# Linear attention whose keys' exponentials are taken from the turned context, with outputs one step behind their sums, and feed-forward scales moved into its middle steps

## The reference

```python
# stage 1: q from x (normalized), k and v from the context
qh = softmax(qh, axis=3)                     # over the 32 channels of a head
kh = softmax(kh, axis=1)                     # over the 1024 positions
kvs = einsum('bnhd,bnhe->bhde', kh, vh)
out = einsum('bnhd,bhde->bnhe', qh, kvs)     # x = x + tanh(g_xattn[0]) * out
# stage 2: feed-forward with 4-bit weights and low-rank parts
y1 = x1 @ Wg + x1 @ g_lora_a @ g_lora_b ; y2 = x1 @ Wu + x1 @ u_lora_a @ u_lora_b
x3 = relu(y1) * y2 ; y3 = x3 @ Wd + x3 @ d_lora_a @ d_lora_b
# stages 3 and 4: auto-correlation attention and a linear layer
```

## Time and profile before

| | us |
|---|---|
| median of 3 runs | 2186.99 (2183.91 to 2187.79) |
| profiled execution | 2186.56 |
| its span | 2184.8 |
| PE busy | 2050.8 (94%) |
| ACT busy | 1176.9 (54%) |
| DVE busy | 1094.9 (50%) |
| POOL busy | 663.8 (30%) |

### The profile page before, as it was taken

One profiled execution on the slowest core, in us unless ns is written; L12 is line 12 of the kernel. 1 busy time (PEld: TensorE's weight loads), 2 busy tenths in 40 slices (PEclk: granted clock), 3 DMA queues, 4 the chain that ended last, 5 costly groups with the idle time before them and its releaser, 6 DMA issues. The chain is left out here.

```text
span 2184.8 us, 25848 instructions
## 1 busy us (share of the span) xinstructions
PE 2050.8 (94%) x9634; PEld 1022.4 (47%) x9634; DVE 1094.9 (50%) x1935; ACT 1176.9 (54%) x1843; POOL 663.8 (30%) x640
## 2 busy tenths in 40 slices
PE   7986999999999999999999999999865799999997
PEld 5773444444444444444444444444322455555543
DVE  6774252433425243342524234252546788888862
ACT  6994756556565655656566565657122344443421
POOL 3432212112121211212121111212125666677641
PEclk9997999999999999999999999999876899999999
DMA  6632211121111112111111111110300011111000
GB/s 224 201 121 68 64 49 54 49 64 49 49 54 50 54 50 63 49 49 54 56 50 54 55 49 49 54 58 20 121 29 10 29 39 49 49 46 37 25 27 31
DMA packets 58493, 128.37 MB, mean 59 GB/s; under 512 B 8704, under 2 KB 9344, under 8 KB 58368
## 3 DMA queue, kind: packets, MB, share of 16 engines
q1 hardware_dynamic: 58368, 126.72, 18.1%
HBM read 118.30 MB, written 8.39 MB: 58 GB/s over the span
## 5 line engine op out<-in xcount | busy, mean ns | idle before, releaser
L664 ACT ACTIVATE first<-first 128x512 f32<-128x512 int32 x1008 | 632.7, 628 | 28.0
L896 PE MATMUL ps_ring<-xT_hi,gu_hi 128*128 128x512 f16 x1376 | 522.1, 379 | 1.7 <-POOL gu_lo L736 1.7
L896 PE MATMUL ps_ring<-xT_hi,gu_lo 128*128 128x512 f16 x1376 | 521.9, 379 | 0.0
L896 PE MATMUL ps_ring<-xT_lo,gu_hi 128*128 128x512 f16 x1376 | 521.8, 379 | 0.0
L805 DVE SCALAR_TENSOR_TENSOR X<-ps_ring,ffn_gain,X 128x512 f32<-128x512 f32 x352 | 259.9, 749 | 168.9 <-PE ps_ring L919 168.8
L786 DVE SCALAR_TENSOR_TENSOR wt<-first,w_scale,absm 128x512 f32<-128x512 f32 x132 | 98.8, 749 | 479.1 <-ACT first L664 478.1
L736 POOL TENSOR_TENSOR gu_lo<-wt,gu_hi 128x512 f16<-128x512 f32 x88 | 102.6, 1166 | 746.7 <-ACT gu_hi L670 746.7
L919 PE MATMUL ps_ring<-dn_hi,hid_hi 128*128 128x512 f16 x704 | 270.0, 384 | 0.0
L919 PE MATMUL ps_ring<-dn_hi,hid_lo 128*128 128x512 f16 x704 | 269.7, 383 | 0.0
L919 PE MATMUL ps_ring<-dn_lo,hid_hi 128*128 128x512 f16 x672 | 256.4, 382 | 0.0
L896 PEld LDWEIGHTS ps_ring<-xT_hi,gu_lo 128*128 128x128 f16 x1376 | 134.5, 98 | 163.1 <-issue 0.8
(11 more groups left out here) (203 smaller groups left out, 2673.4 us busy)
## 6 DMA issues: line engine op xcount, KB each, us to landing
first<-in_codes SPq DMA_DIRECT2D x132, 256.0 KB, 2.8
absm<-in_absmax SPq DMA_DIRECT2D x264, 128.0 KB, 3.1
X<-in_x SPq DMA_DIRECT2D x16, 512.0 KB, 4.1
c_in<-in_ctx SPq DMA_DIRECT2D x16, 512.0 KB, 5.0
cT<-in_ctxT SPq DMA_DIRECT2D x16, 512.0 KB, 3.5
xT_hi<-in_ctx SPq DMA_DIRECT2D x8, 1024.0 KB, 7.2
out<-X SPq DMA_DIRECT2D x16, 512.0 KB, 3.3
gu_hi<-in_w SPq DMA_DIRECT2D x8, 512.0 KB, 3.6
```

Source lines behind the costliest of these rows:

```text
L664: act.activation(level[u % 2][:], codes[u % RING] if k == 0 else level[u % 2][:], ACT.Prelu, bias=bias, scale=scale, alpha=alpha).then_inc ...
L896: mm = pe.matmul(o[:], w[c][:, m, k, :], xx[:, k, ts], start=(q == 0), stop=(q == 3 * KD - 1))
```

## The change

- Keys: the maximum cm goes to PE, which spreads it over all partitions (`maxima`), ACT copies it out (cmx), POOL subtracts it from the turned context (`less_max`, new, 128x1024), and ACT takes the exponentials straight into ekT (`keys`). The eight turns of ek and the copy to ekT are gone. The key sums come from a column of ones behind each block of cT, as column 128 of the product.
- The head sums of eq take four columns of blk for each block, and lie in psE. The turned inverse sums have a buffer rT of their own, and eq has three copies.
- POOL multiplies eq in the step after its sums (`eqn` of tile i-1 in step i). DVE forms the second offset of tile i-2 in step i, after xT_lo and ahead of rS; `prepare` is split, and the first offset stands at the end of the step. ACT's xn is one step later too.
- The scales' parts move: squares in step 7, reductions in step 8, PE and DVE gathering in steps 9 and 10, POOL's roots in step 11, DVE's chain in step 12; their loads are issued ahead of tile 4.

```diff
 pool_part:  -        if i == TILES:
             +        if i == AT + 3:                       # AT = 8
 act_part:   -        if i == TILES - 2:
             +        if i == AT - 1:
 dve_part:   -        if i == TILES - 1:   +        if i == AT:
             -        if i == TILES:       +        if i == AT + 1: (top, diag)  and  if i == AT + 2: (every)
             -        if i == TILES + 1:   +        if i == AT + 4:
@@ SP
-                sp.dma_start(cT[h][:], io["ctxT"][b, h]).then_inc(cT_in[h], 16)
+                sp.dma_start(cT[h][:, :, 0:P], io["ctxT"][b, h].rearrange("p (k j) -> p k j", k=KD)).then_inc(cT_in[h], 16)
...
-                        sp.wait_ge(ek_done, b * 2 + h - 1)
+                        sp.wait_ge(cmax_done, b * 2 + h - 1)
@@ POOL
+            def less_max(i, h):
+                pool.wait_ge(cT_in[h], (i // 2) * 16 + 16)
+                pool.wait_ge(cmx_done, i + 1)
+                after(pool, kv_mm, i - 1)
+                pool.tensor_tensor(ekT[h][:].rearrange("p (k j) -> p k j", k=KD), cT[h][:, :, 0:P],
+                                   cmx[h][:].unsqueeze(1).to_broadcast([P, KD, P]), ALU.subtract).then_inc(sub_done, 1)
             def step(i, h):
                 if exists(i - 1):
-                    rsqrt(i - 1, 1 - h, mv2, ve2, rstd2, mv2_done, ve2_done, rstd2_done)
-                if exists(i):
-                    pool.wait_ge(turned_done, i + 1)
-                    pool.tensor_tensor(eq[h][:], rSx[:], eq[h][:], ALU.mult).then_inc(eqn_done, 1)
+                    pool.wait_ge(turned_done, i)
+                    pool.tensor_tensor(eq[(i - 1) % 3][:], rT[:], eq[(i - 1) % 3][:], ALU.mult).then_inc(eqn_done, 1)
+                if exists(i + 1):
+                    less_max(i + 1, 1 - h)
                 if exists(i + 2):
                     rsqrt(i + 2, h, mv, ve, rstd, mv_done, ve_done, rstd_done)
+                if exists(i - 1):
+                    rsqrt(i - 1, 1 - h, mv2, ve2, rstd2, mv2_done, ve2_done, rstd2_done)
...
             for h in range(2):
                 rsqrt(h, h, mv, ve, rstd, mv_done, ve_done, rstd_done)
+            less_max(0, 0)
@@ ACT, new order of step(i): queries(i+1), xn(i-2), maxima(i+1), rSx(i), first_kinks(i), keys(i+1), turned(i) into rT, xT_hi(i-2)
+            def maxima(i, h):
+                act.wait_ge(cmb_mm, i + 1)
+                after(act, sub_done, i - 1)
+                act.activation(cmx[h][:], ps_max, ACT.Copy).then_inc(cmx_done, 1)
+            def keys(i, h):
+                act.wait_ge(sub_done, i + 1)
+                act.activation(ekT[h][:], ekT[h][:], ACT.Exp).then_inc(ek_done, 1)
@@ PE, new order of step(i): sums(i), product(i), maxima(i+1), out(i-1), turned sums(i), xT(i-2)
+            def maxima(i, h):
+                pe.wait_ge(cmax_done, i + 1)
+                after(pe, rS_done, i)
+                pe.matmul(ps_max, cm[h][:].to_broadcast([P, P]), ident[:], start=True, stop=True).then_inc(cmb_mm, 1)
...
+                        mm = pe.matmul(ps_sums[:, k * HR:(k + 1) * HR], eq[i % 3][:, k * P:(k + 1) * P], blk[:, 0:P:ROWS0], start=True, stop=True)
...
+                        mm = pe.matmul(ps_kv, ekT[h][:, k * P:(k + 1) * P], cT[h][:, k, :], start=(k == 0), stop=(k == KD - 1))
@@ DVE
             def prepare(i, h):
+                dve.wait_ge(ctx_in[h], (i // 2) * 16 + 16)
+                after(dve, cmb_mm, i - 1)
+                dve.reduce_max(cm[h][:], c_in[h][:], AX.X).then_inc(cmax_done, 1)
+                dve.wait_ge(x_in[h], (i // 2) * 16 + 16)
                 stats(i, h, st, mv, stats_done, mv_done)
...
             def step(i, h):
                 (xT_lo of tile i-3, as before)
+                if exists(i - 2):
+                    offset(i - 2, h, mv2, rstd2, nmr2, rstd2_done, nmr2_done)
                 if exists(i):
                     dve.wait_ge(sums_mm, i + 1)
+                    dve.reciprocal(rS[h][:], ps_sums).then_inc(rS_done, 1)
+                if exists(i + 2):
+                    prepare(i + 2, h)
+                if exists(i):
+                    dve.wait_ge(kv_mm, i + 1)
+                    dve.reciprocal(rks[h][:], ps_kv[:, P:P + 1]).then_inc(rks_done, 1)
+                    dve.wait_ge(rks_done, i + 1)
+                    dve.scalar_tensor_tensor(kvm[h][:], ps_kv[:, 0:P], rks[h][:], blk[:], ALU.mult, ALU.mult).then_inc(kvm_done, 1)
                 (X and its statistics of tile i-1, as before)
+                if exists(i + 2):
+                    offset(i + 2, h, mv, rstd, nmr, rstd_done, nmr_done)
 
             for h in range(2):
                 prepare(h, h)
+            for h in range(2):
+                offset(h, h, mv, rstd, nmr, rstd_done, nmr_done)
```

More of the change, by code:

```diff
@@ L221, in dve_part, with read, left @@
             dve.wait_ge(step, 30)
-    return sp_part, pool_part, act_part, pe_part, dve_part
+    def read(engine):
+        engine.wait_ge(step, 3)
+    def left(pe, i):
+        if i == AT + 2:
+            pe.wait_ge(step, 7)
+        if i == AT + 3:
+            pe.wait_ge(step, EVERY)
+    return sp_part, pool_part, act_part, pe_part, dve_part, read, left
 def exists(i):
@@ L309, in _ @@
                 for b in range(1, B):
+                    if b == 2:
+                        scales_sp(sp)
                     if b == 3:
@@ L375, in step @@
                 def step(i, h):
-                    if exists(i):
-                        after(act, kv_mm, i - 1)
-                        act.wait_ge(ekT_mm, i + 1)
-                        act.activation(ekT[h][:], psE[:], ACT.Copy).then_inc(ekT_done, 1)
-                    first_kinks(i)
-                    if exists(i):
-                        after(act, eqn_done, i)
+                    if exists(i + 1):
+                        queries(i + 1, 1 - h)
+                    if exists(i - 2):
+                        after(act, xT_mm, i - 3)
+                        act.wait_ge(nmr2_done, i - 1)
+                        settle(act)
+                        act.activation(xn[h][:], X[:, i - 2, :], ACT.Identity, scale=rstd2[h][:], bias=nmr2[h][:]).then_inc(xn_done, 1)
+                    if exists(i + 1):
+                        maxima(i + 1, 1 - h)
+                    if exists(i):
+                        after(act, rS_mm, i)
                         act.wait_ge(rS_done, i + 1)
@@ L401, in step @@
                                        ACT.Copy, scale=LN_SCALE).then_inc(hi_done, 1)
-                exponentials(0, 0)
+                queries(0, 0)
+                maxima(0, 0)
+                keys(0, 0)
                 act.wait_ge(gates_in, 32)
@@ L427, in step @@
                         for n in range(2):
-                            mm = pe.matmul(psO[:, n * BANK:(n + 1) * BANK], kvm[1 - h][:], eq[1 - h][:, n * BANK:(n + 1) * BANK], start=True, stop=True)
+                            mm = pe.matmul(psO[:, n * BANK:(n + 1) * BANK], kvm[1 - h][:], eq[(i - 1) % 3][:, n * BANK:(n + 1) * BANK], start=True, stop=True)
                         mm.then_inc(out_mm, 1)
                     if exists(i):
-                        pe.wait_ge(ekT_done, i + 1)
-                        pe.wait_ge(cT_in[h], (i // 2) * 16 + 16 if isinstance(i, int) else (i - h) * 8 + 16)
-                        for k in range(KD):
-                            mm = pe.matmul(psE[:, 0:P], ekT[h][:, k * P:(k + 1) * P], cT[h][:, k * P:(k + 1) * P], start=(k == 0), stop=(k == KD - 1))
-                        mm.then_inc(kv_mm, 1)
                         pe.wait_ge(rSx_done, i + 1)
+                        after(pe, turned_done, i)
                         for k in range(KD):
@@ L448, in _ @@
                 pe.wait_ge(const_in, 32)
+                pe.wait_ge(ones_set, 2)
+                maxima(0, 0)
                 run(pe, step, scales_pe)
```

119 lines of the change are left out of this document (53 added, 66 removed).

## The result

The changed kernel takes 2214.53 us, the median of four runs (2207.84 to 2219.71). The kernel before took 2187.39 beside it, also of four (2183.91 to 2191.63). The ratio of after to before is 1.0109, with an interval of 1.0085 to 1.0133. The forecast was slower, at 2196, with a range up to 2202: the time is above that range. The kernel did get slower and the held offset is there, but the size is not: the medians are 27 us apart, and the ratio puts the loss at 24 us (19 to 29), where the forecast had 9. The profiled execution is the fastest of the four, at 2207.84.

A forecast was written before the change was run, and what follows sets the result against it. ACT bound the 9.32 us step, PE 0.2 us behind. After: 31.9 to first X addition, 146.7 for steps with scales, 9.9 at the end: 188.5 against 178.6, 9.9 more, rounded to 9.5: 2196 us, range 2182 to 2202.

The forecast's parts named there:

- the held offset: DVE's second offset always falls into POOL's product and is held until its end, 2.30 us instead of 0.16; chance 0.60.
- first X addition: Stage's start: later offset, table load and POOL's subtraction delay the first X addition by about 6.5 us (5.5 to 7.5).
- The ring: Regular step: chain from one POOL product's end through DVE to the next product's end sets the step, 9.7 against 9.32 us.
- the first rival: Regular step: offset not held, ACT sets steps of 8.4 us, stage 173.8 us, time 2182 us; chance 0.18.
- the second rival: In the prediction's list: offset held in some steps only, mean step 9.05 us, time 2188.5 us; chance 0.12.
- PE ... is not the bound and I price this at zero: Regular step: PE's busy time falls below 8 us, so its changed work costs no time.
- the third rival: Subtraction 3.0 us, loads stalling the start, PE longer at half clock there: 2 us each, time 2202 us; chance 0.10.
- The scales: Scales' parts in middle steps: reductions +1.2 us in step 8, roots +1.0 and DVE's chain +2.1 in step 12.
- The loads: Regular step: cT is needed a step earlier but a full step covers its load, priced at zero; uncovered, 1 to 2 us.
- The subtraction: POOL's added 128x1024 subtraction in each regular step takes 2.37 us, with 2.0 and 3.0 as ends.
- fourth rival: PE's head sums with 4 columns do not get shorter; this changes no time in any case, as PE has room.
- The end: From the last X addition to the stage's end: about 9.9 us instead of 12.4, 2.5 less.

The follow-up runs named there:

- the last experiment: The kernel before the change with its offsets in the one-input form (scalar operand) and nothing else changed: 2181.94 us, ratio 0.9973 to the kernel before.

## Why the prediction was right in kind and wrong in size

The forecast put the stage's end at 188.5; the profiled execution has 202.8. Its terms against what was measured:

| term | forecast | measured |
|---|---|---|
| first X addition | +6.5 | +9.5 |
| regular step, held | 9.7 | 9.69 to 9.79 in five of fifteen |
| steps 1, 2 and 5 | 3 x 9.7 | 32.7, so +3.6 |
| steps 8 to 12, over 5 x 9.7 | +4.3 | +9.6 |
| last three steps | 26.0 | 28.0 |
| from last X addition to the end | 9.9 | 10.1 |

The 14.3 us between the two ends can be read from DVE's waits in after, since DVE sets the steps; these sums are estimates from one execution. Waits for PE's output at half clock make about 8: 1.55 ahead of the first addition, 0.98 and 0.45 in steps 2 and 5, 1.8 in step 11, 1.33 in step 12 and 1.8 in step 15. Waits for the context make about 5: the queries' start 1.5 later than forecast, 1.87 in step 1 and 1.70 in step 9. About 1 us is left over.

- **The held offset: right.** The ring came out at 9.70 us against 9.7. With the hold gone the step is 8.57 where the first rival had 8.4 (its time of 2182 did not follow, though: 2207.77, for the reasons below; and the prediction's sentence that calls the unheld case the second rival means this first one), and the comparison in which only the offset's form differs puts the hold's price at 18.4 us of the steps. The Trainium skill's rule ("SBUF — State Buffer", section "Who interferes with whom") fits both: the form with one input in SBUF passes in 0.20 us under a running product, the form with two takes until its end. The scalar operand lies in SBUF too; the traces show only that it does not bring the hold.
- **"PE ... is not the bound and I price this at zero": the step that failed.** It took PE's busy time at full clock. That was so before: PE was busy for 8.54 of 9.32 us, and the granted clock stood at 1.00 from 20 to 160 us. In after it is busy for 7.94 of 9.70. PE's gap ahead of its turn for the maximum grew to 1.8 us in the regular step shown and to 3 us and more around the scales, and the granted clock fell to 0.82 to 0.91 from 100 us on. A group behind a gap then takes up to 1.8 us longer just where it ends the wait of DVE's X. That is in the start (sixteen matmuls in 3.6 to 3.8 us), in the output of steps 11 and 12 (+1.8 and +1.6), and in the last step, 10.33 instead of 8.5. Filling the gaps took the terms of steps 2, 5 and 11 away, but added as much elsewhere, so no run isolates the 8 us. The forecast did say half clock of the last turns, but for the end alone, and the third rival had a longer half clock at the start, at 2 us.
- **The scales: their own work was priced about right.** Steps 8 to 12 came 5.3 us dearer than forecast, by the two causes around this one. The reductions made step 8 longer by 1.0 us, with 1.2 forecast. Step 9 is the wait for the context. Step 11 is 2.9 over 9.7; 1.8 of that is the output's half clock, and 1.1 is left for the roots, with +1.0 forecast, and the offset got through as said (0.15 us at 143.25). Step 12 is 3.8 over; DVE's 1.33 us for PE's output leave 2.5 for the chain, with +2.1 forecast. Its held instruction is a later one (L210) and not its first, as the forecast had it. In the kernels without the hold the same work has less shade: 2.2 us for the reductions (10.8 less 8.58), and 8.6 for roots and chain, some of it clock, against 2.5 and 3.7 in the first rival.
- **The loads: a zero that holds only for a long step.** In after DVE waits 2.35 and 1.05 us for the context ahead of the first addition (before, 1.94 us for tile 1's x), and 1.87 and 1.70 in steps 1 and 9. SP issued these last two loads right behind the scales' inputs (33.01 to 34.18) and behind the low-rank loads (113.48 to 115.11); with the low-rank loads moved away, step 9 has no such wait. Landing times of the profile's DMA part went up from 4.1 to 5.0 us for x, 5.0 to 5.9 for the context and 3.5 to 4.4 for cT:
```profile
DMA packets 72828, 128.35 MB, mean 58 GB/s; under 512 B 8704, under 2 KB 25728, under 8 KB 72704
X<-in_x SPq DMA_DIRECT2D x16, 512.0 KB, 5.0
c_in<-in_ctx SPq DMA_DIRECT2D x16, 512.0 KB, 5.9
cT<-in_ctxT SPq DMA_DIRECT2D x16, 512.0 KB, 4.4
```
  Packets under 2 KB were 9344 before. Once the hold was gone, these waits grew to 12.2 us, and issuing two tiles ahead ended those in the steps. The third rival had the loads, the start and the clock together, at 2 us each; the clock and the loads alone came at about 8 and 5.
- **The subtraction** takes 2.17 to 2.22 us, within its bounds. **The sums with 4 columns** (fourth rival) take 1.85 us against 1.97 for sixteen, so they did not get shorter and it changed nothing, as said.
- **The end: right**, 2.3 us less against 2.5.
- **The rest** moved by 3.1 us in the profiled execution, over the 1 us I allowed. Over all runs profiled here it took 2003 to 2012 us at the same instruction counts, with no order that I can tie to an edit. So 24.2 us of the stage's loss are shown by the profile; that the medians differ by 27 is not resolved to a microsecond.

What stays open: why the clock falls in some regular steps and not in others, what it costs when nothing else changes, why the stretch behind the stage varies, and the lower median of the last experiment.

## What to carry to other kernels

A short instruction with two SBUF inputs on DVE took up to 2.3 us here, until the end of the POOL product beside which it fell. So when a change reorders POOL, look for each of these and try the form with a scalar operand: that decided 18.4 us of the steps here. When a step gets a new bound, price the others again for the gaps that it leaves: PE kept its full clock and the loads came in time in the regular steps of 9.32 us, and neither held in the changed kernel. Side work belongs where the pipeline drains: the same roots and chain cost 8.6 us in the middle steps and next to nothing in the last.

## What was not expected of the hardware

- A POOL power of 128x12 elements takes 2.28 us, nearly as long as its product over 128x1024 (2.37), while one of 128x1 takes 0.57.
- Sixteen f32 matmuls with 4 moving columns take 1.85 us, those with 128 take 1.97: the loads of their 128x128 weights are busy for 1.86 us of it.
- DVE's offset with its second factor as a scalar takes 0.20 us under a running POOL product, against 1.14 to 2.30 for the same arithmetic with two tensors.
- Filling PE's idle time raised the granted clock of the regular steps (1.00 from 40 to 120 us, where it had fallen to 0.83 in three of eight stretches of 10 us) and did not shorten the whole (2216.36 against 2214.53).
